# Waits of VectorE on its own results at four places of the tile loop of a two-layer graph network

## The chip, the cores and the metric

The kernel runs on one core of a Trainium2 chip. The metric is the device time of one execution in microseconds (us), from start to end, as the median of several executions. TensorE is PE, VectorE is DVE, ScalarE is ACT, GpSimd is POOL and SyncE is SP in the profile.

## The reference

Two layers pass messages over a graph of 6250 nodes with 206,250 edges (100,000 in both directions and one loop per node), 48 features a node. Shortened to what is computed:

```python
# layer 0
deg = segment_sum(ones, src)                       # self loops added again
h = x + segment_sum(x[src] * rsqrt(deg)[src] * rsqrt(deg)[dst], dst)
h = layernorm(h)
# layer 1
gate = silu(edge_attr @ W1.T + b1) @ W2.T + b2     # 40 -> 48 -> 48, per edge
gate += sum(emb[z[src]] * (emb[z[dst]] @ adaptW.T), -1)
cw = where(d < 6, 0.5 * (cos(pi * d / 6) + 1), 0)
msg = gate * h[dst] * (cw * mult[dst])
agg = segment_sum(msg, src) / segment_sum(mult[dst], src)
out = layernorm(layernorm_affine(h + agg) + h)
```

The edges come sorted by dst.

## The kernel before

The program has three stages. The first (to about 240 us) turns the node and edge lists into keys, counts degrees and fills a table of node rows in HBM (`table`). The second is a loop over NT = 101 tiles of 128 x 16 edges. The third adds up what the loop left in HBM (`slots`) for 51 buckets of nodes and normalizes.

**The tile loop.** `over_tiles` runs a list of steps per engine, each step with a lag: in turn t a step with lag 4 works on tile t - 4. Each engine has a list of its own, in a hand-written order, and executes it strictly in order; semaphores tie the lists together. The steps that matter:

- POOL (L711 to L731) does two things only. `gather` issues 16 indirect DMAs a tile, each of which fetches 128 table rows into `slot` (L718); it first waits until the sums, the gate and the product of the tile six back are done, and for the tile's indices. `scatter` (L726) writes the routed rows of tile t - 6 to `slots` with one indirect DMA. Indirect DMAs are made up by POOL itself.
- SP (L661 to L707) issues the plain loads in the order `index` (the indices of the coming gathers, L666), `load` (edge attributes), `rows`, `weigh`, and from the 47th tile on `early_rows` (L701), which waits until PE's early sum before it is done.
- PE (L863): `layer1`, `pick` (node rows by the one-hot `oh_t`), `layer2`, `routes` (112 matmuls with the one-hots `oh_r`, L815), `early_sum` (21 matmuls with `eoh`, L836), `ranks` (with `oh_b`), and last `total`, the matmul of the gathered rows with the one-hot of dst `oh_d` (L850), which waits for all 16 gathers.
- ACT (L1029) moves results out of PSUM: `ssum` (L898), `got` and `parts` (L943, L949), `routed` (L888), `emine` (L975, the places of the early rows).
- DVE (L1255) makes the one-hots and the products. In a turn, after `normalize` (odd tiles only, a chain of some 17 tiny instructions): `step_at`, `oh_d` (`onehots`, L1041, 128 x 2048 elements), `oh_b` (`buckets`, L1046), eight `oh_r` of 128 x 896 (`route_onehots(0)`, L1083), `sidx`, from the 47th tile on `add_early` and `early_onehots` (L1170: `eoh` in two pieces of 16 and 5 columns), `less_first`, `less_high(0)` (L1209), `product(1)` (L1188 to L1201), `less_second`, `places` (`oh_t`, L1051), `less_high(1)`, `less_middle(0)` (L1217), eight more `oh_r` (`route_onehots(1)`), `less_middle(1)`; then `spots`, `keys` and `product(0)` of the next turn.

**Early rows.** From the 47th tile on, each turn also takes the first 96 of the 256 places of one of the 51 buckets out of `slots`: SP loads them (`erows`), ACT copies the places, DVE makes the one-hot `eoh`, PE sums, ACT copies the sum out, DVE adds it up. The rest of the places is done in the third stage.

**Waits.** `e.wait_ge(sem, n)` holds the engine's next instruction back until the semaphore has come to n. `wait_apart(e, sem, n, passed)` (L80) puts an increment of a semaphore that nobody reads behind the wait. DVE waits for its own results in `product` (`own`, `gate_used`) and `normalize` (`chain`), where one instruction reads what the one before wrote. Between the one-hots it doesn't; there is nothing that the next reads of the last.

## Time and profile before

| | |
|---|---|
| three timed executions | 3001.81, 3028.74, 3037.04 us; median 3028.74 |
| the profiled execution | 3017.23 us, its span in the trace 3015.4 us |
| first gather of the tile loop starts at | 241.60 us |
| last gather of the tile loop starts at | 2712.32 us |
| busy time of DVE, PE, POOL, ACT | 2404.1, 2240.8, 2132.0, 1396.7 us |
| granted clock of TensorE, mean | 0.847 of full speed |

In a timeline row stand the start, the duration, engine, line, operation, what it writes and reads, the shapes, how many instructions were merged (x8), and in brackets the idle time of its engine before it with what ended that. "issue" there means that nothing which the profile shows was waited for. DMA-issuing instructions of POOL are shown with the time that POOL itself spent on them; that the data has landed is shown by who waits for it.

### The profile page before, as it was taken

The page shows a single profiled execution, that of the slowest core. Times are in us where ns is not written, and L with a number is a line of the kernel's source. Part 1 is how long each engine was busy: PE and PEld are TensorE (multiplying, and loading weights), DVE is VectorE, ACT ScalarE, POOL GpSimd, SP SyncE. Part 2 cuts the span into 40 slices and gives each one's busy share as a digit, 9 for nine tenths or more (in the row PEclk, how much of TensorE's full clock was granted, in tenths as well). Part 3 has the DMA queues.
Part 4 walks back from the last instruction along what each step waited for, and adds up shares of the span by engine and source line. Part 5 has one row for each costly group of instructions (what it writes and reads, how often), then busy time and mean ns, then how long its engine had stood idle before and what let it go on. Part 6 is the DMA issues. An engine that isn't in the chain of part 4 may idle for free.

```text
span 3015.4 us, 73281 instructions
## 1 busy us (share of the span) xinstructions
PE 2240.8 (74%) x25807; PEld 1910.9 (63%) x25909; DVE 2404.1 (80%) x5426; ACT 1396.7 (46%) x2928; POOL 2132.0 (71%) x1852
## 2 busy tenths in 40 slices
PE   6980477777777777876787777878778777878675
PEld 5870355566666666665566666766666666767674
DVE  9994477777787877877788888888778878888798
ACT  7982244444444444544444444444444444445123
POOL 7406777877777777778777777777777777770255
PEclk8665688888888878888889898988889988899898
DMA  8405233334444444443344454545445544453896
GB/s 315 156 0 164 62 100 111 111 114 128 116 118 123 113 121 121 118 123 100 109 145 146 144 151 140 159 142 159 132 132 156 153 131 150 146 148 118 336 389 221
DMA packets 167498, 438.96 MB, mean 146 GB/s; under 512 B 85302, under 2 KB 85302, under 8 KB 147446
## 3 DMA queue, kind: packets, MB, share of 16 engines
q1 hardware_dynamic: 96266, 233.49, 23.4%
q0 software_dynamic: 67888, 194.98, 22.4%
q10 hardware_dynamic: 3004, 5.90, 0.6%
q8 instruction: 220, 3.60, 0.5%
q14 instruction: 120, 0.98, 0.1%
HBM read 291.23 MB, written 142.99 MB: 144 GB/s over the span
## 4 chain that ended last, share of the span: by engine, by line
POOL 33%; PE 19%; issue 16%; DVE 14%; DMA 7%; ACT 1%; DVEq 0%; POOLq 0%; ACTq 0%; SPq 0%
POOL slot L718 32%; PE acc L1588 4%; PE route L815 4%; DMA erows<-slots 4%; PE pwin L771 3%; DVE oh_r L1083 3%; DMA slot<-table,gidx 3%; PE phid L741 3%; PE gate L753 2%; PE pwin L850 2%; POOL slots L726 1%; DVE val L1194 1%; DVE eoh L1170 1%; PE pwin L836 1%; DVE val L1197 1%
## 5 line engine op out<-in xcount | busy, mean ns | idle before, releaser
L718 POOL DMA_INDIRECT slot<-table,gidx x1616 | 1819.1, 1126 | 634.2 <-issue 624.7
L815 PEld LDWEIGHTS route<-parts,oh_r 128*128 128x128 bf16 x11312 | 761.7, 99 | 88.1 <-issue 63.5
L815 PE MATMUL route<-parts,oh_r 128*128 128x148 bf16 x11312 | 810.1, 232 | 3.4 <-DVE parts L1217 3.0
L1083 DVE TENSOR_SCALAR oh_r<-iota_r,spot 128x896 bf16<-128x896 f16 x1616 | 613.5, 449 | 69.4 <-PE route L815 69.2
L888 ACT ACTIVATE routed<-route 128x444 bf16<-128x444 f32 (+1 forms) x1010 | 507.9, 513 | 255.1 <-PE route L815 241.6
L850 PE MATMUL pwin<-slot,oh_d 128*128 128x144 bf16 x1616 | 173.5, 282 | 428.1 <-DMA slot<-table,gidx 396.9
L850 PEld LDWEIGHTS pwin<-slot,oh_d 128*128 128x128 bf16 x1616 | 152.4, 156 | 452.2 <-issue 294.1
L771 PEld LDWEIGHTS pwin<-win,oh_t 128*128 128x128 bf16 x4848 | 257.1, 115 | 181.1 <-issue 95.6
L741 PE MATMUL phid<-attr,w 80*96 80x512 f32 x404 | 285.1, 796 | 47.6 <-issue 47.1
L771 PE MATMUL pwin<-win,oh_t 128*128 128x80 bf16 (+1 forms) x4848 | 271.4, 224 | 50.5 <-ACT ssum L898 45.6
L1188 DVE TENSOR_TENSOR prod<-slot,got 128x256 f32<-128x256 f32 x202 | 84.2, 417 | 241.1 <-ACT parts L949 241.1
L753 PE MATMUL gate<-w,hid 97*128 97x96 f32 x1616 | 249.2, 303 | 1.6 <-ACT hid L876 1.6
L943 ACT ACTIVATE got<-pwin 128x640 f32<-128x640 f32 x202 | 142.0, 703 | 221.8 <-PE pwin L771 221.1
L753 PEld LDWEIGHTS gate<-w,hid 97*128 97x128 f32 x1616 | 223.9, 214 | 3.5 <-ACT hid L876 2.8
L726 POOL DMA_INDIRECT slots<-routed,sidx x101 | 119.6, 1184 | 111.3 <-ACT routed L888 73.1
L956 ACT ACTIVATE parts<-val 128x384 bf16<-128x384 f32 x202 | 104.5, 517 | 197.5 <-DVE val L1201 197.5
L876 ACT ACTIVATE hid<-phid,b1c 96x512 f32<-96x512 f32 x202 | 137.6, 681 | 121.9 <-PE phid L741 119.1
L327 ACT ACTIVATE by_col<-oh_hi 128x832 bf16<-128x832 bf16 x101 | 179.4, 1797 | 16.3 <-DVE oh_lo L467 11.6
L1170 DVE TENSOR_TENSOR eoh<-number,emine 128x2048 bf16<-128x2048 bf16 x102 | 102.8, 1057 | 97.0 <-ACT emine L975 96.3
L1588 PE MATMUL acc<-rows,onehot 128*128 128x147 bf16 x1785 | 135.9, 239 | 52.9 <-issue 34.5
L1588 PEld LDWEIGHTS acc<-rows,onehot 128*128 128x128 bf16 x1785 | 130.4, 143 | 58.5 <-issue 58.4
L964 ACT ACTIVATE parts<-val 128x384 bf16<-128x384 f32 x202 | 108.4, 537 | 74.7 <-DVE val L1209 73.4
(226 smaller groups left out, 3221.1 us busy)
## 6 DMA issues: line engine op xcount, KB each, us to landing
rows<-slots SPq DMA_DIRECT2D x51, 1295.0 KB, 9.1
oh_t<-dst_row SPq DMA_DIRECT2D x101, 512.0 KB, 5.5
erows<-slots SPq DMA_DIRECT2D x51, 777.0 KB
attr<-in_edge_attr SPq DMA_DIRECT2D x101, 320.0 KB
slots<-zeros SPq DMA_DIRECT2D x53, 518.0 KB
slot<-table,gidx POOLq DMA_INDIRECT x1616
table<-tab SPq DMA_DIRECT2D x3, 676.0 KB, 5.5
weight_t<-weights SPq DMA_DIRECT2D x101, 8.0 KB
```

Of the source, the lines that this page charges most:

```text
L327: e.activation(by_col[:, s % OR], oh_hi[:, s % OR].rearrange("p b g -> p g b"), ACT.Copy).then_inc(laid, 1)
L718: e.indirect_dma_start(out=slot[:, s, g, :], out_offset=None, in_=table0, in_offset=bass.IndirectOffsetOnAxis(ap=gidx[:, s, g:g + 1], axis ...
L726: e.indirect_dma_start(out=perm, out_offset=bass.IndirectOffsetOnAxis(ap=sidx[:, s:s + 1], axis=0), in_=routed[:, s % 2, :], in_offset=Non ...
L741: e.matmul(phid[:, :], w1[:, :], attr[:, s % 2, 512 * m:512 * (m + 1)], start=True, stop=True).then_inc(hidden, 1)
L753: mm = e.matmul(gate[:, 2 * C * k:2 * C * (k + 1)], hid[:, P * c:P * (c + 1)], w2[:, :], start=True, stop=True)
L771: mm = e.matmul(pwin[:, g // 4, first:first + n], oh_t[:, s % 2, m * HC + g, :], win[:, s, AT[k]:AT[k] + n], start=(k == 0), stop=(k == 2) ...
L815: mm = e.matmul(route[:, (NPH * m + phase) % 2, RC * (j - a):RC * (j - a + 1)], oh_r[:, c, slot_of, :], parts[:, s % 2, c, :], start=(c == ...
L850: mm = e.matmul(sums, oh_d[:, s % 2, :, g], rows[:, g, :], start=(g == 0), stop=(g == G - 1))
L888: e.activation(routed[:, s % 2, RC * (HS * m + a):RC * (HS * m + b)], route[:, (NPH * m + phase) % 2, 0:RC * (b - a)], ACT.Copy).then_inc( ...
L943: e.activation(got[:, m].rearrange("p (b k) c -> p b k c", b=2), by_bank[:, :, :, 0:WX], ACT.Copy)
L1083: oh = e.tensor_scalar(oh_r[:, c], iota_r[:, :, :], spot[:, s % 2, c:c + 1], None, ALU.is_equal)
L1588: mm = e.matmul(acc[:, b % 2, 0:3 * MW], onehot[:, b % OS, :, c], rows[:, b % RS, c, 0:3 * MW], start=(c == 0), stop=(c == COLS - 1))
```

## The change

DVE waits at four places until its own last instruction is done, each time with `wait_apart`: behind `oh_d` (every tile), behind the last `oh_r` of `route_onehots(1)` (every tile), behind `less_high(0)` (every tile), and between the two pieces of `eoh` (51 visits of buckets), for which a semaphore `epart_made` is new. No operand, no size and no order of steps changes.

```diff
--- before.py
+++ after.py
@@ -621,8 +621,8 @@
                                      "ranked", "placed", "routing", "rows_ok_f", "picked",
                                      "got_ok", "gated", "own", "gate_used", "val_ok", "high", "rested_f",
                                      "mid", "split_ok", "stepped", "group_rows", "ones_ok"))
-            erows_in, ecopied, emade, esummed = (
-                sem(n) for n in ("erows_in", "ecopied", "emade", "esummed"))
+            erows_in, ecopied, emade, esummed, epart_made = (
+                sem(n) for n in ("erows_in", "ecopied", "emade", "esummed", "epart_made"))
             (dst_at, all_at, v, a_own, w_ready, w_turned, w_out, rest_ok, weighed, query_r) = (
                 sem(n) for n in ("dst_at", "all_at", "v_p", "a_own_p", "w_ready", "w_turned", "w_out", "rest_ok",
                                      "weighed", "query_r"))
@@ -1040,6 +1040,7 @@
                         e.wait_ge(summed, t - 1)
                     e.tensor_tensor(oh_d[:, s % 2], number[:, :, :], bc_mid(w16[:, bass.ds(t * G, G)], P),
                                     ALU.is_equal).then_inc(ohd, 1)
+                    wait_apart(e, ohd, t + 1, passed)
 
                 def buckets(i, s):
                     t = U * i + s
@@ -1083,6 +1084,8 @@
                             oh = e.tensor_scalar(oh_r[:, c], iota_r[:, :, :], spot[:, s % 2, c:c + 1], None,
                                                  ALU.is_equal)
                         oh.then_inc(ohr, 1)
+                        if m == 1:
+                            wait_apart(e, ohr, 2 * t + 2, passed)
                     return step
 
                 def normalize(i, s):
@@ -1165,10 +1168,13 @@
                     wait_apart(e, ecopied, 2 * v + 1, passed)
                     if not isinstance(v, int) or v > 0:
                         e.wait_ge(esummed, v)
-                    for a in range(0, ECOLS, G):
+                    for k, a in enumerate(range(0, ECOLS, G)):
                         b = min(a + G, ECOLS)
                         oh = e.tensor_tensor(eoh[:, :, a:b], number[:, :, 0:b - a], bc_mid(emine[:, a:b], P),
                                              ALU.is_equal)
+                        if b < ECOLS:
+                            oh.then_inc(epart_made, 1)
+                            wait_apart(e, epart_made, (ECOLS - 1) // G * v + k + 1, passed)
                     oh.then_inc(emade, 1)
 
                 def add_early(i, s):
@@ -1208,6 +1214,8 @@
                         e.wait_ge(high, n + 1)
                         e.tensor_tensor(val[:, m], val[:, m], parts[:, s % 2, m * HC:(m + 1) * HC, 0:C],
                                         ALU.subtract).then_inc(rested, 1)
+                        if m == 0:
+                            wait_apart(e, rested, n + 1, passed)
                     return step
 
                 def less_middle(m):
```

How DVE's queue stands in a turn with early rows. Names are the tiles written and read; `[waits ...]` lists the semaphores that the row waits for; ISA and REGISTER_ALU rows compute addresses and counts. DVE, from the step rows of the groups to the first `oh_r`, before:

```order
L1063 ISA [waits group_rows]
L1063 TENSOR_TENSOR step_at<-iota_f,rstart_t 52x128
L1041 ISA [waits summed_f]
L1041 TENSOR_TENSOR oh_d<-number,w 128x2048
L1046 ISA
L1046 TENSOR_TENSOR oh_b<-number,bkt 128x816
L83 ISA [waits placed]
L1083 TENSOR_SCALAR oh_r<-iota_r,spot 128x896 [waits routing]
```

and now:

```order
L1064 ISA [waits group_rows]
L1064 TENSOR_TENSOR step_at<-iota_f,rstart_t 52x128
L1041 ISA [waits summed_f]
L1041 TENSOR_TENSOR oh_d<-number,w 128x2048
L83 REGISTER_ALU
L1047 ISA [waits ohd]
L1047 TENSOR_TENSOR oh_b<-number,bkt 128x816
L83 ISA [waits placed]
L1084 TENSOR_SCALAR oh_r<-iota_r,spot 128x896 [waits routing]
```

The wait for `ohd`, which `oh_d` increments, now stands behind `oh_d`, ahead of the address computation of `oh_b`.

DVE, from the early one-hots to `product(1)`, before:

```order
L1170 TENSOR_TENSOR eoh<-number,emine 128x128x16 [waits ecopied,esummed]
L1170 TENSOR_TENSOR eoh<-number,emine 128x128x5
L1141 REGISTER_ALU
L1142 TENSOR_TENSOR hm<-hm,win 128x48 [waits win_h]
L1209 TENSOR_TENSOR val<-val,parts 128x384 [waits high]
L1187 REGISTER_ALU
L1188 TENSOR_TENSOR prod<-slot,got 128x256 [waits got_ok]
```

and now:

```order
L1173 TENSOR_TENSOR eoh<-number,emine 128x128x16 [waits ecopied,esummed]
L83 REGISTER_ALU
L1173 TENSOR_TENSOR eoh<-number,emine 128x128x5 [waits epart_made]
L1144 REGISTER_ALU
L1145 TENSOR_TENSOR hm<-hm,win 128x48 [waits win_h]
L1215 TENSOR_TENSOR val<-val,parts 128x384 [waits high]
L1193 REGISTER_ALU [waits rested_f]
L1194 TENSOR_TENSOR prod<-slot,got 128x256 [waits got_ok]
```

The second piece of `eoh` now waits for the first (`epart_made`), and the row ahead of `prod` waits for `val` (`rested_f`).

DVE, from `less_middle(0)` to the next turn's `spot`, before:

```order
L1217 TENSOR_TENSOR parts<-val,parts 128x8x48 [waits mid]
L83 REGISTER_ALU
L1083 TENSOR_SCALAR oh_r<-iota_r,spot 128x896 [waits routing]
L1083 TENSOR_SCALAR oh_r<-iota_r,spot 128x896 x7
L1217 TENSOR_TENSOR parts<-val,parts 128x8x48 [waits mid]
L1056 TENSOR_REDUCE spot<-rank 128x16 [waits ranked]
```

and now:

```order
L1225 TENSOR_TENSOR parts<-val,parts 128x8x48 [waits mid]
L83 REGISTER_ALU
L1084 TENSOR_SCALAR oh_r<-iota_r,spot 128x896 [waits routing]
L1084 TENSOR_SCALAR oh_r<-iota_r,spot 128x896 x7
L1225 TENSOR_TENSOR parts<-val,parts 128x8x48 [waits ohr,mid]
L1057 TENSOR_REDUCE spot<-rank 128x16 [waits ranked]
```

`less_middle(1)`, the second `parts`, now also waits for the last `oh_r` (`ohr`).

## Rows read from the trace of the kernel before

**Rows 1.** The page: the chain that ended last, by engine.
```profile
POOL 33%; PE 19%; issue 16%; DVE 14%; DMA 7%; ACT 1%; DVEq 0%; POOLq 0%; ACTq 0%; SPq 0%
```
**Rows 2.** Groups of POOL by line, 241 to 1670 us, then 1670 to 2712 us.
```profile
L718 POOL DMA_INDIRECT slot<-table,gidx x945 | 1065.7, 1128 | 409.9 <-issue 405.7 <-DVE val L1194 3.7 <-DMA gidx<-src_pid 0.6
L726 POOL DMA_INDIRECT slots<-routed,sidx x53 | 59.8, 1128 | 16.1 <-issue 16.1
...
L718 POOL DMA_INDIRECT slot<-table,gidx x671 | 753.5, 1123 | 224.3 <-issue 219.0 <-DMA gidx<-src_pid 5.0 <-DVE val L1194 0.3
L726 POOL DMA_INDIRECT slots<-routed,sidx x41 | 52.1, 1271 | 12.5 <-issue 11.9 <-DMA gidx<-src_pid 0.6
```
**Rows 3.** The gather's line and the one-hot of dst: durations min/median/max in ns.
```profile
L718 POOL DMA_INDIRECT slot<-table,gidx x1616: 938/1012/5685, 241.6 to 2712.3; - x180
...
L1041 DVE TENSOR_TENSOR oh_d<-number,w x101: 1206/1209/1226, 278.4 to 2674.9; 128x2048 bf16<-128x2048 bf16 x101
```
**Rows 4.** Timeline of POOL: the first and the last gather that start inside an oh_d.
```profile
279.57 1.97 POOL L718 DMA_INDIRECT slot<-table,gidx  x1 [0.30 <-issue]
...
2675.87 1.52 POOL L718 DMA_INDIRECT slot<-table,gidx  x1 [0.30 <-issue]
```
**Rows 5.** Timeline of DVE and POOL around two gathers that start inside oh_d.
```profile
1216.66 1.21 DVE L1041 TENSOR_TENSOR oh_d<-number,w 128x2048 bf16<-128x2048 bf16 x1
1217.11 1.58 POOL L718 DMA_INDIRECT slot<-table,gidx  x1 [0.30 <-issue]
...
1409.05 1.21 DVE L1041 TENSOR_TENSOR oh_d<-number,w 128x2048 bf16<-128x2048 bf16 x1
1409.86 5.67 POOL L718 DMA_INDIRECT slot<-table,gidx  x1 [0.30 <-issue]
1410.19 0.57 DVE L1046 TENSOR_TENSOR oh_b<-number,bkt 128x816 bf16<-128x816 bf16 x1
...
1414.30 0.41 DVE L1188 TENSOR_TENSOR prod<-slot,got 128x256 f32<-128x256 f32 x1
```
**Rows 6.** Waits: who waited for whom, us in total, times, longest us.
```profile
PE pwin L850 <- DMA slot<-table,gidx: 396.9, 94, 18.9
DVE prod L1188 <- ACT parts L949: 241.1, 51, 18.9
DVE eoh L1170 <- ACT emine L975: 96.3, 32, 6.4
PEld pwin L771 <- ACT ssum L898: 74.8, 43, 4.9
DVE oh_r L1083 <- PE route L815: 69.2, 43, 2.9
```
**Rows 7.** Timeline of DVE inside normalize, with waits on its own results.
```profile
1508.53 0.27 DVE L1114 SCALAR_TENSOR_TENSOR y<-y,dinv,base 128x48 f32<-128x48 f32 x1 [0.19 <-DVE y L1113]
...
1509.19 0.18 DVE L1119 BATCH_NORM_AGGREGATE mv<-stat 128x2 f32<-128x6 f32 x1 [0.15 <-DVE stat L1117]
```
**Rows 8.** Timeline around less_high(0) and product(1) without a wait between.
```profile
1267.29 0.55 DVE L1209 TENSOR_TENSOR val<-val,parts 128x384 f32<-128x384 f32 x1
1267.54 1.44 POOL L718 DMA_INDIRECT slot<-table,gidx  x1 [0.30 <-issue]
1267.75 0.41 DVE L1188 TENSOR_TENSOR prod<-slot,got 128x256 f32<-128x256 f32 x1
```
**Rows 9.** Timeline of POOL: a gather that starts inside the last oh_r before less_middle(1).
```profile
2171.06 1.59 POOL L718 DMA_INDIRECT slot<-table,gidx  x1 [0.30 <-issue]
```
**Rows 10.** Timeline of POOL: gathers that start inside the first piece of eoh.
```profile
1517.60 2.52 POOL L718 DMA_INDIRECT slot<-table,gidx  x1 [0.30 <-issue]
...
1540.91 1.93 POOL L718 DMA_INDIRECT slot<-table,gidx  x1 [0.30 <-DMA gidx<-src_pid]
```
**Rows 11.** A late tile: POOL in the timeline, then a piece of the chain.
```profile
2214.65 1.57 POOL L718 DMA_INDIRECT slot<-table,gidx  x1 [2.74 <-issue]
...
2205.72 7.94 DMA erows<-slots
```

## The prediction

> **What bounds the kernel now.** I read the page's shares and its chain first. The page alone misleads: VectorE is busy longest (2404 us in the table above), and the chain gives POOL only 33% and PE 19% [rows 1]. The tile loop runs from the first gather at 241 us to the last at 2712 us, and in it no engine is full by its busy time. So I looked at what POOL does between its instructions. A gather (L718) lasts 0.94 us at least (938 ns [rows 3]), and 0.30 us "issue" stands before it [rows 4, 5]: with rounding, one each 1.25 us. That 0.30 is there before nearly every gather: 945 gathers and 53 scatters in the first stretch take 1065.7 + 409.9 + 59.8 + 16.1 = 1551 us, more than the 1429 us only because the 122 us wait ahead of the first gather is counted; without it, 1429 of 1429. In the second stretch 753.5 + 224.3 + 52.1 + 12.5 = 1042 of 1042, of which 224.3 - 671 x 0.30 = 23 us are real waits [rows 2]. POOL is full by its issue pace. A tile's 16 gathers and a scatter cost 17 x 1.25 = 21.2 us undisturbed, and a tile takes 2471 / 101 = 24.5.
>
> The difference is gathers that last longer than 0.94: min 938, median 1012, max 5685 ns [rows 3]. The mean of 1126 gives (1126 - 940) x 1616 = 300 us in all. I laid the 1616 gathers against VectorE's timeline. A gather that starts inside an instruction of one-input reduction, of `val<-gate,logit` or of the short normalizing ones lasts 0.94. One that starts inside a one-hot or a product with two SBUF inputs lasts longer, by just the time until that instruction is nearly done. Of the 100 that start inside an `oh_d` (the first at 279.57, the last at 2675.87 [rows 4]) the extras add up to 99 us. And the hold does not always end with the instruction. At 1217.11 a gather inside `oh_d` lasts 1.58: taking 0.94 off its end, it was let go at 1217.75, `oh_d` + 1.09; at 1409.86, 0.81 us into the same instruction, one lasts 5.67 and comes free only when `oh_b`, all eight `oh_r`, `sidx`, `hm`, `val` and `prod` have run [rows 5]. There are 8 of these (6 over 5.6 us, 2 over 5.1). Nearly all the instructions it sat through overlap the next one (`oh_d` lasts 1.21, `oh_b` starts at +1.14); it comes free near the end of `prod`, the first of them behind which VectorE waits for its own result.
>
> PE has slack: 397 us of waits for gathers, 94 times, 4.2 a tile. VectorE has (241.1 + 96.3 + 69.2) / 101 = 4.0 us a tile of waits for others [rows 6].
>
> **The change, part by part.** Nothing is removed or reordered. 101 + 51 + 101 + 101 = 354 waits of VectorE on its own last result are added. What is queued behind each: `oh_b`, the second `eoh` piece, `less_middle(1)`, `product(1)`, on which ranks, the early sum, the second half of routes and the gate wait.
>
> *Price of one.* The trace has such waits: `mv` starts 0.15 us after `stat` ends, where a wait and a bare semaphore increment stand between; `y` L1114, with an address to be computed after the wait, starts 0.19 us late [rows 7]. Without a wait the next starts 0.09 us early (1267.29 + 0.55 against 1267.75 [rows 8]). So 0.24 to 0.28, I take 0.25, since in other pairs the overlap is 0.07: 354 x 0.25 = 88 us of VectorE, 0.87 a tile, out of 4.0 of slack. From below a wait could cost nothing, where VectorE would wait for others anyway; from above 0.19 + 0.94, if a gather that slips into the gap held VectorE as long as it runs. The second I hold unlikely: `oh_d` takes 1206 to 1226 ns in all 101 [rows 3], though gathers run across it.
>
> *Gain of one.* I take each gather that is held past the end of an instruction which now gets a wait behind it, and let it go at that end:
> `oh_d` (releases at +1.09): 35 of 56 held gathers in tiles 0 to 58 give 46.7 us, of it 6 x 4.4 + 2 x 3.4 = 33 from the eight long ones; 21 of 41 later give 10.4.
> `less_high(0)` before `product(1)`: 16 gathers, all like the one at 1267.54, 1.44 long [rows 8], 0.3 each: 5.0, all in the first part.
> The last `oh_r` before `less_middle(1)`: like 2171.06, 1.59 long [rows 9]: 12 give 4.9, 9 later give 3.7.
> Between the `eoh` pieces: at 1517.60 a gather is held through both (2.52), at 1540.91 only through the first (1.93) [rows 10]: 3 give 1.8 early, 7 later 5.3.
> Sum: 58.4 us in tiles 0 to 58, 19.4 after. That is a replay with unchanged phases. If gathers fell at random (an arrival inside `oh_d` then waits 1.09 / 2 with chance 1.09 / 1.25, so 0.48 us a tile against 0.99 now) the whole first part would give 45. I take 52.
>
> *Who is late next.* In the first part (to about 1670 us) POOL never waits, and PE has its 4.2 us a tile. VectorE's 4.0 less 0.87 less about 0.9 of gain leaves 2.2, so POOL stays the bound and the 52 us arrive. From the sixtieth tile a ring of another kind is about as slow as POOL: early sum, SP's early rows, their DMA (7.9 us at 2205.72 [rows 11]), `emine`, `eoh` (96 us idle before it [rows 6]), `less_high(0)`, `product(1)`, ScalarE, `pick`, early sum. There the gathers' index load hangs behind SP's early rows, POOL itself waits 2.74 us at 2214.65 [rows 11]; PE's loads wait so 43 times, 74.8 us [rows 6]. 27 of the 39 tiles 59 to 97 have this idle. Two of the added waits lie on that ring (in `eoh`, behind `less_high(0)`): + 0.5 us a tile. Where it decides (27 tiles) + 13 us and nothing of the 19 comes; where POOL decides a third of 19 comes. I put the second part at + 0, from - 19 to + 20. After the last gather the loop drains five tiles through PE and VectorE, of whose chain VectorE is under half: 5 x 0.87 x 0.6 = + 3 us. The last stage is untouched.
>
> Sum: - 52 + 0 + 3 = - 49. The profiled execution took 3017.2 us (span 3015.4): 2968. The median shown is 3028.7, 11.5 above it, in a spread of 35; I put the forecast between 2968 and 3028.7 - 49 = 2980, at 2975, 1.8% down.
>
> **A rule that speaks against it.** In the trace a gather is delayed by `oh_d`, a TENSOR_TENSOR of VectorE [rows 5]. The Trainium skill (SBUF — State Buffer, Who interferes with whom) says that a two-input VectorE instruction contends with GpSimd instructions that read SBUF, and infers that descriptor generation, which writes, is spared by `tensor_tensor`; it also says that the loser is blocked for the whole instruction, no longer. By the first nothing would be gained at `oh_d` and `eoh`; the trace disagrees (99 us in 100 gathers). By the second a gather goes free when the instruction ends, wait or none, and the gain is nil; the trace agrees for 1217.11 and disagrees for 1409.86. This second is a rival below.
>
> **The rivals.**
> *The late ring takes it back.* For it: the 23 us that POOL already waits, and the 43 waits for `ssum`. Against: 59 tiles lie ahead of it. First part - 45, second + 0.6 x 39 = + 23, drain + 4: 3017 - 18 = 2999, and 3011 by the median.
> *The gap frees nothing.* What keeps a gather out for 4.7 us could be its own retry or a phase, not the missing gap. For it: at + 0.70 in `oh_d` gathers are released at + 1.09 with the same overlap, at + 0.81 not. Against: no gather that starts in `val` L1197 or `prod`, which have a self-wait behind them, is held longer than 0.42. Then only the price is left: ring + 0.3 x 39 = 12, drain 4: 3017 + 16 = 3033.
> *VectorE becomes the bound (slower).* If a gather in the gap keeps the port for its 0.94 us, each wait costs 1.19, 3.5 x 1.19 = 4.2 us a tile. It decides from 4.0 a tile on in the first part, at once in the ring. Second part + 2 x 1.19 x 39 = + 93, first + 0.2 x 59 = + 12, less a gain of 45, drain + 12: 3017 + 72 = 3089. Against it: `oh_d`'s constant duration.
>
> **The numbers.** Forecast 0.60, late ring 0.20, nothing freed 0.13, VectorE bound 0.07. A measurement of this kernel can tell about 1%, 30 us: faster means under 2998. The forecast lies there but for 0.04, of the late ring 0.08: together 0.64. Slower (over 3059) has the last rival and a little of the third: 0.09. Within 1%: 0.27. The range takes - 19 in the second part and 58 in the first as its low end (2940), the late ring and part of "nothing freed" as the high one (3030).
>
> **What the profile after would show.** Right: the longest gather drops from 5.7 to about 2 us, the mean of L718 from 1126 to 1080 ns, gathers inside `oh_d` end by + 1.09, `oh_b` starts 0.15 to 0.2 after `oh_d` ends, the loop ends near 2665. The ring shows as POOL's "issue" idle above 0.30 and waits for `ssum` growing after 1650 us. Wrong: gathers still held past `oh_d` (nothing freed); `oh_b`, `prod` starting 0.9 late or VectorE's waits for others near zero (VectorE bound).

## The result, and the profile after

The changed kernel takes 3043.9 us (median of 20 runs, 3029.0 to 3049.4), the kernel before 3029.5 us (20 runs, 3001.8 to 3037.0). The ratio is 1.0051, with a 95% interval of [1.0036, 1.0067]: half a per cent slower, where 1.8% faster was forecast. 3043.9 lies outside the predicted range of 2940 to 3030.

The page of the changed kernel, first its chain by engine, which answers to [rows 1], then groups of instructions with busy time, mean ns of one, and the idle time before them:

```profile
POOL 28%; PE 19%; DVE 19%; issue 16%; DMA 7%; ACT 2%; DVEq 1%; SPq 0%; ACTq 0%; POOLq 0%
...
L718 POOL DMA_INDIRECT slot<-table,gidx x1616 | 1770.5, 1096 | 697.4 <-issue 658.0
...
L1084 DVE TENSOR_SCALAR oh_r<-iota_r,spot 128x896 bf16<-128x896 f16 x1616 | 605.3, 446 | 55.2 <-PE route L815 55.2
```

POOL has lost 5 points of the chain and VectorE has won 5. A gather lasts 1096 ns on average instead of 1126, so the gathers as such became 48 us cheaper in all. POOL's groups by line, 241 to 1635 us and then 1635 to 2702 us, answer to [rows 2]:

```profile
L718 POOL DMA_INDIRECT slot<-table,gidx x944 | 1025.4, 1086 | 411.7 <-issue 409.2 <-DVE val L1200 2.1 <-DMA gidx<-src_pid 0.3
L726 POOL DMA_INDIRECT slots<-routed,sidx x53 | 59.1, 1115 | 16.1 <-issue 16.1
...
L718 POOL DMA_INDIRECT slot<-table,gidx x656 | 725.8, 1106 | 278.2 <-issue 241.2 <-DMA gidx<-src_pid 37.0
L726 POOL DMA_INDIRECT slots<-routed,sidx x42 | 48.8, 1162 | 12.8 <-issue 12.8
```

In the first stretch the gathers' busy time fell from 1065.7 to 1025.4 us and nothing else grew by over 2 us: POOL is still full by its issue pace but for 6 us, and the gain arrives. In the second the gathers are shorter too (1106 against 1123 ns), but POOL's idle time is now 278.2 - 656 x 0.30 = 81 us above the pace, where it was 23 us. POOL is no longer always the bound there. The stretches of the loop side by side, divided at the first gather of the tiles with index 51, 59 and 100 (us, and behind the counts the granted clock); first the changed kernel:

```profile
240.89:1438.26 1197.37, 856.48 (x9741) 716.78 (x9741) 903.62 (x2254) 529.13 (x1166) 935.00 (x861) 0.84 0.41 118
1438.26:1635.45 197.19, 153.15 (x1770) 130.35 (x1769) 158.77 (x383) 87.67 (x205) 149.51 (x137) 0.88 0.46 138
1635.45:2702.41 1066.96, 840.32 (x9431) 720.66 (x9428) 858.55 (x2049) 466.87 (x1089) 773.59 (x698) 0.85 0.47 139
```

and the kernel before at the same tiles:

```profile
241.60:1474.30 1232.70, 859.87 (x9690) 721.09 (x9739) 904.35 (x2265) 531.46 (x1168) 970.30 (x861) 0.84 0.40 114
1474.30:1669.92 195.62, 153.97 (x1803) 130.49 (x1809) 158.44 (x383) 89.67 (x205) 154.16 (x136) 0.89 0.47 140
1669.92:2688.87 1018.95, 814.34 (x9348) 693.26 (x9389) 842.63 (x2039) 466.87 (x1084) 786.74 (x697) 0.87 0.49 146
```

The loop starts 0.7 us earlier and reaches tile 59 after 1394.6 instead of 1428.3 us. With the earlier start that is 34.5 us won at tile 59. The 41 tiles behind it take 1067.0 instead of 1019.0 us: 48.0 lost. From there to the end another 7.0 are lost. - 34.5 + 48.0 + 7.0 = + 20.5, the difference of the two spans (3035.9 and 3015.4).

Durations in ns (min/median/max), which answer to [rows 3]:

```profile
L718 POOL DMA_INDIRECT slot<-table,gidx x1616: 938/954/3474, 240.9 to 2725.3; - x180
...
L1041 DVE TENSOR_TENSOR oh_d<-number,w x101: 1206/1209/1226, 277.9 to 2690.7; 128x2048 bf16<-128x2048 bf16 x101
```

Of the ten gathers over 3 us one is left, in the drain. Laid against VectorE's timeline, 95 gathers start inside `oh_d`, with 57.7 us of extra time (before: 100 with 99.2), and none of them has more than 0.97 us extra (before: up to 4.73). The four added waits in one late tile, the timeline of VectorE, answer to [rows 5, 7, 8]:

```profile
1704.19 0.58 DVE L1047 TENSOR_TENSOR oh_b<-number,bkt 128x816 bf16<-128x816 bf16 x1 [0.25 <-DVE oh_d L1041]
...
1715.28 0.88 DVE L1173 TENSOR_TENSOR eoh<-number,emine 128x640 bf16<-128x640 bf16 x1 [0.15 <-DVE eoh L1173]
1716.76 0.42 DVE L1194 TENSOR_TENSOR prod<-slot,got 128x256 f32<-128x256 f32 x1 [0.22 <-DVE val L1215]
1724.14 0.56 DVE L1225 TENSOR_TENSOR parts<-val,parts 128x384 bf16<-128x384 f32 x1 [0.15 <-DVE oh_r L1084]
```

With the overlap that is gone (0.07 to 0.09) a wait costs 0.32 behind `oh_d`, 0.31 behind `less_high(0)`, 0.23 to 0.29 at the other two. And at the end of some loop turns there is something that no row of before had led me to expect. VectorE's timeline there, and the same with the line of `spot` as a whole:

```profile
1617.76 1.53 DVE L1084 TENSOR_SCALAR oh_r<-iota_r,spot 128x896 bf16<-128x896 f16 x4
1619.45 0.56 DVE L1225 TENSOR_TENSOR parts<-val,parts 128x384 bf16<-128x384 f32 x1 [0.15 <-DVE oh_r L1084]
1622.65 1.01 DVE L1057 TENSOR_REDUCE spot<-rank 128x16 f32<-128x816 f32 x1 [2.64 <-issue]
...
  issue: 31.8, 11
```

`spot` is the first instruction of a loop turn of six tiles. 11 times VectorE stands idle for 2.4 to 4.9 us ahead of it, waiting for nothing that the profile shows, 31.8 us in all; before it did so 3 times, for 2.3 us. The 11 are the tiles with index 18, 24, 30, 36 and then 54, 60 and so on to 90. For VectorE `over_tiles` writes out the first 17 tiles' turns and 6 in the middle one by one, and puts the others into two loops of 5 and of 8 turns of six tiles: there are 11 jumps back, and the idle stretches stand behind just these. The rows of waits, last, answer to [rows 6]:

```profile
PE pwin L850 <- DMA slot<-table,gidx: 288.8, 78, 18.5
...
DVE prod L1194 <- ACT parts L949: 154.2, 26, 19.0
PE pwin L771 <- ACT ssum L898: 150.1, 54, 5.7
PEld pwin L771 <- ACT ssum L898: 131.8, 48, 5.5
...
DVE eoh L1173 <- ACT emine L975: 102.2, 33, 5.8
```

PE's waits for gathers shrink by 108 us, and its weight loads' waits for `ssum` grow from 74.8 to 131.8 us. I read that as the ring of the late part (early sum, early rows, `eoh`, `less_high(0)`, `product(1)`) coming later than POOL more often than before.

### The profile page after: what moved, and what is told of

Read it like the earlier page. It is cut to its first block, busy times and chain, and to the rows that moved or that the text cites. A ratio compares the mean times of both kernels' runs of the same rounds, so it can differ in the third digit from the quotient of the medians.

```text
span 3035.9 us, 73850 instructions
## 1 busy us (share of the span) xinstructions
PE 2263.1 (75%) x25909; PEld 1936.3 (64%) x25909; DVE 2422.0 (80%) x5426; ACT 1390.8 (46%) x2928; POOL 2079.4 (68%) x1852
## 4 chain that ended last, share of the span: by engine, by line
POOL 28%; PE 19%; DVE 19%; issue 16%; DMA 7%; ACT 2%; DVEq 1%; SPq 0%; ACTq 0%; POOLq 0%
POOL slot L718 27%; DMA erows<-slots 5%; PE route L815 5%; PE acc L1596 4%; DVE oh_r L1084 4%; PE pwin L771 4%; DVE eoh L1173 3%; PE gate L753 2%; PE phid L741 2%; DVE val L1200 1%; PE pwin L836 1%; POOL slots L726 1%; DVE val L1203 1%; DVE logit L1197 1%; DVE prod L1194 1%
## 5 line engine op out<-in xcount | busy, mean ns | idle before, releaser
L718 POOL DMA_INDIRECT slot<-table,gidx x1616 | 1770.5, 1096 | 697.4 <-issue 658.0
L1084 DVE TENSOR_SCALAR oh_r<-iota_r,spot 128x896 bf16<-128x896 f16 x1616 | 605.3, 446 | 55.2 <-PE route L815 55.2
L771 PEld LDWEIGHTS pwin<-win,oh_t 128*128 128x128 bf16 x4848 | 283.4, 124 | 270.4 <-ACT ssum L898 131.8
L771 PE MATMUL pwin<-win,oh_t 128*128 128x80 bf16 (+1 forms) x4848 | 298.9, 237 | 155.7 <-ACT ssum L898 150.1
L850 PE MATMUL pwin<-slot,oh_d 128*128 128x144 bf16 x1616 | 151.9, 259 | 320.8 <-DMA slot<-table,gidx 288.8
L850 PEld LDWEIGHTS pwin<-slot,oh_d 128*128 128x128 bf16 x1616 | 136.1, 151 | 341.8 <-issue 200.3
L741 PE MATMUL phid<-attr,w 80*96 80x512 f32 x404 | 271.1, 759 | 49.3 <-issue 37.8
L753 PE MATMUL gate<-w,hid 97*128 97x96 f32 x1616 | 267.3, 318 | 1.6 <-ACT hid L876 1.6
L753 PEld LDWEIGHTS gate<-w,hid 97*128 97x128 f32 x1616 | 241.5, 229 | 3.3 <-ACT hid L876 2.8
L1173 DVE TENSOR_TENSOR eoh<-number,emine 128x2048 bf16<-128x2048 bf16 x102 | 109.5, 1073 | 110.1 <-ACT emine L975 102.2
```

The lines of the kernel that those rows point to most:

```text
L718: e.indirect_dma_start(out=slot[:, s, g, :], out_offset=None, in_=table0, in_offset=bass.IndirectOffsetOnAxis(ap=gidx[:, s, g:g + 1], axis ...
L741: e.matmul(phid[:, :], w1[:, :], attr[:, s % 2, 512 * m:512 * (m + 1)], start=True, stop=True).then_inc(hidden, 1)
L753: mm = e.matmul(gate[:, 2 * C * k:2 * C * (k + 1)], hid[:, P * c:P * (c + 1)], w2[:, :], start=True, stop=True)
L771: mm = e.matmul(pwin[:, g // 4, first:first + n], oh_t[:, s % 2, m * HC + g, :], win[:, s, AT[k]:AT[k] + n], start=(k == 0), stop=(k == 2) ...
L850: mm = e.matmul(sums, oh_d[:, s % 2, :, g], rows[:, g, :], start=(g == 0), stop=(g == G - 1))
L1084: oh = e.tensor_scalar(oh_r[:, c], iota_r[:, :, :], spot[:, s % 2, c:c + 1], None, ALU.is_equal)
```

## The experiments

All kernels below are the changed kernel with a condition on its four waits. `in_late` is true in the loops that also serve the early rows, from tile `EARLY_FROM`. Ratios are to runs of the kernel before on the same chip. Chips and medians of before: 3019.6 us for the first four kernels and again, on a second chip, for the next four.

| kernel | waits left | median us | ratio and interval |
|---|---|---|---|
| changed | all four | 3043.9 | 1.0051 [1.0036, 1.0067] |
| first_only | `oh_d`, `oh_r`, `less_high(0)`; early part only | 2998.5 | 0.9935 [0.9910, 0.9960] |
| late_off | `oh_d`, `oh_r`; late part only | 3037.7 | 1.0056 [1.0030, 1.0082] |
| late_on | `eoh`, `less_high(0)`; late part only | 3040.8 | 1.0069 [1.0043, 1.0094] |
| ohd_only | `oh_d`, all tiles | 2994.5 | 0.9923 [0.9898, 0.9948] |
| ohr_last | `oh_r`, last tile of a turn | 3028.0 | 1.0040 [1.0017, 1.0064] |
| ohr_others | `oh_r`, the other five tiles | 3032.9 | 1.0060 [1.0037, 1.0082] |
| four_others | all but `oh_r` in the last tile | 3020.9 | 1.0014 [0.9991, 1.0037] |
| best_a | `oh_d` all; `less_high(0)` and `oh_r` (not the last tile) early only | 2972.3 | 0.9859 [0.9831, 0.9887] |

**Which part, which waits.**

```diff
# first_only (the eoh wait is taken out)
-                    wait_apart(e, ohd, t + 1, passed)
+                    if not in_late(i, s):
+                        wait_apart(e, ohd, t + 1, passed)
...
-                        if m == 1:
+                        if m == 1 and not in_late(i, s):
                             wait_apart(e, ohr, 2 * t + 2, passed)
...
-                        if m == 0:
+                        if m == 0 and not in_late(i, s):
                             wait_apart(e, rested, n + 1, passed)
```

> The three waits of every tile stand only in tiles 0 to 46, before the early rows begin; none stands later. Theory ring (the first part is bound by POOL, and the gain there is real; the late part loses it): the stretch up to the 52nd tile's first gather takes 1197 us as in the changed kernel (1233 before), the rest is as before, about 1.2% under the kernel before (2995). Rival run (the 35 us of the first part are only a chance of phase, and the late part makes up for a POOL that is ahead by waiting more): no faster than before, 3025 to 3035, with POOL's waits above 0.30 grown in the late part.

Measured: 0.65% faster (0.9935), 2998.5 us. With the waits of the early part alone the change gains; the tiles behind 59 lose nothing (1009.5 us, taken as above). The mark of 1197 us up to tile 51 was missed: 1217.4, some half of the gain, because the waits end at tile 45.

```diff
# late_off (less_high(0) and eoh waits are taken out)
+                    if in_late(i, s):
                         wait_apart(e, ohd, t + 1, passed)
...
-                        if m == 1:
+                        if m == 1 and in_late(i, s):
                             wait_apart(e, ohr, 2 * t + 2, passed)
```

> Only in the late tiles (from the 47th on), and only the two waits that do not lie on the ring of the early rows: behind oh_d and behind the last oh_r. Theory ring (only what lies on early sum, load, emine, eoh, less_high(0), product(1), pick counts): these two cost nothing, 3029, within 0.3% of before. Rival queue (in the late part VectorE's whole queue is the bound, every wait is paid in full wherever it stands): 0.31 + 0.23 us a tile, 54 tiles, +29 us less 10 of gathers let go: +20 to +29, 3050 to 3058.

```diff
# late_on (oh_d and oh_r waits are taken out, the eoh wait stays)
-                        if m == 0:
+                        if m == 0 and in_late(i, s):
                             wait_apart(e, rested, n + 1, passed)
```

> Only in the late tiles, and only the two waits on the ring: between the pieces of eoh and behind less_high(0). Theory ring: 0.29 + 0.31 us a tile, 51 tiles, +30 us, and since the changed kernel lost 48 us there, up to +48: 3059 to 3077. Rival queue: +30 us, 3059, and together with the run with the other two waits the sum makes up the changed kernel's late loss.

```diff
# ohd_only (the other three are taken out)
                     wait_apart(e, ohd, t + 1, passed)
```

> Only the wait behind oh_d, in all tiles. The replay gave 80% of the first part's gain to it. Theory ring: 27 us gained early, nothing lost late: 3002, 0.9% under before. Rival queue: 27 gained, 0.31 x 54 = 17 lost: 3019, 0.3% under. In both no gather that starts inside oh_d lasts over 2.05 us.

Measured: late_off 0.56% and late_on 0.69% slower than before, ohd_only 0.77% faster. late_off was expected within 0.3% by the one theory and at + 20 to + 29 us by the other, and late_on at + 30 or more by both: neither theory foresaw + 17 and + 21. ohd_only came out as the theory of the ring had it, with 27.4 us gained at tile 59 and no gather inside `oh_d` over 1.9 us. So both pairs of waits lose in the late part, and not by way of `oh_d`: with its wait alone the last 41 tiles take 1016.6 us, not more than before. first_only, late_off and late_on divide the change's waits among them, each wait in just one: 0.9935 x 1.0056 x 1.0069 = 1.0060, and the changed kernel has 1.0051 [1.0036, 1.0067]. The three effects add up: - 20, + 17 and + 21 us. The wait behind `oh_d` stands in late_off from tile 46 on, so part of the early gain is in it: tile 59 starts 16.6 us earlier than before in first_only, 15.8 in late_off and 34.5 in the changed kernel. Two causes were left: the pair on the ring, as the prediction had it, and the wait behind the last `oh_r`, which it had put at no loss. In late_off's trace the idle stretch ahead of `spot` stood again, and what followed it. First VectorE, then PE, then POOL, and the stretch from 1653.80 us with its granted clock (0.58):

```profile
1642.78 1.01 DVE L1066 TENSOR_REDUCE spot<-rank 128x16 f32<-128x816 f32 x1 [2.48 <-issue]
...
1645.54 0.42 DVE L1203 TENSOR_REDUCE logit<-prod 128x8 f32<-128x256 f32 x1 [1.34 <-issue]
...
1653.31 0.58 PE L808 MATMUL rank<-delta_t,step_at 52*128 x2 [4.69 <-DVE step_at L1073]
1653.82 6.34 PE L823 MATMUL route<-parts,oh_r 128*128 128x148 bf16 x56
...
1686.90 1.54 POOL L726 DMA_INDIRECT slot<-table,gidx  x1 [8.70 <-DMA gidx<-src_pid]
...
1653.80:1660.20 6.40, 6.36 (x57) 6.28 (x59) 5.28 (x13) 2.17 (x6) 4.87 (x6) 0.58 0.81 277
```

The same two rows of PE in the kernel before, where the granted clock is 1.00:

```profile
1660.81 0.38 PE L800 MATMUL rank<-delta_t,step_at 52*128 x2 [1.87 <-DVE step_at L1063]
1661.13 3.87 PE L815 MATMUL route<-parts,oh_r 128*128 128x148 bf16 x56
```

VectorE loses 3.8 us, PE idles 4.69 us for `step_at` (before 1.87), the granted clock is 0.58 in the next 6.4 us (near the 1.2 GHz level), and 56 routing matmuls take 6.34 us, 113 ns each (before 3.87 us, 69 ns). POOL's tile 59 lasts 32.8 us instead of 23.6, since at its end POOL waits 8.70 us for its indices. Tiles 59, 65, 77, 83 and 95, five of the seven with index 59, 65 and so on to 95, last 31.8 to 33.1 us in that run.

**The wait at the loop's branch.** The step behind the last `oh_r` of the sixth tile is the last but one of the turn; only `less_middle(1)` stands between its wait and the branch back.

```diff
# ohr_last (the other three are taken out)
-                        if m == 1:
+                        if m == 1 and s == U - 1:
```

> Only the wait behind the last oh_r, and only in the tile whose step stands last in the loop's body (one in six, 17 waits in all, 14 of them right before the branch back). Theory branch: with the wait VectorE's queue is empty when its sequencer comes to the branch, so the branch and the fetch of the next instructions lie bare: 2.4 to 2.7 us idle before spot in each of the 14 turns of the loop, and in the late part the PE behind it idles, its clock falls and a tile of 30 us or more follows; 0.5 to 1% slower, 3035 to 3050. Rival: every wait costs its 0.23 us wherever it stands, 17 x 0.23 = 4 us: 3022 to 3026, no idle before spot.

```diff
# ohr_others (the other three are taken out)
-                        if m == 1:
+                        if m == 1 and s < U - 1:
```

> Only the wait behind the last oh_r, in the other five tiles of six (84 waits). Theory branch: no idle before spot; 84 x 0.23 us are in part hidden, 9 us of gathers let go: within 0.3% of before. Rival (no place is special): five times the effect of the run with the waits in the sixth tile alone, and most of the 26 us a tile of the late part in the run with the two waits off the ring (late tiles 25.5 and more).

```diff
# four_others (the other three stay)
-                        if m == 1:
+                        if m == 1 and s < U - 1:
```

> The changed kernel with one kind of wait left out: behind the last oh_r of the tile that stands last in the loop's body. Theory branch: the first part keeps its gain (52nd tile's first gather at 1440), the late tiles take 25.2 to 25.5 us instead of 26.0, from the two waits on the ring; 3005 to 3020, 0.2 to 0.8% under before and 0.8 to 1.2% under the changed kernel. Rival (the late loss is the sum of all waits): as the changed kernel but for 4 us, 3040.

Measured: the waits at the turn's end alone (ohr_last) cost 0.40%, a little less than the 0.5 to 1% of the theory. The tiles that stand last in a turn have index 5, 11 and so on to 95, so there are 16 such waits and 85 others, not 17 and 84, and 11 of the 16 stand ahead of a jump back, not 14. The idle ahead of `spot` by kernel, the rows of what its engine sat idle for: ohr_last, then first_only; before and the changed kernel had 2.3 us 3 times and 31.8 us 11 times:

```profile
  issue: 27.9, 11
...
  issue: 12.7, 6
```

ohr_others, ohd_only and best_a have no such idle stretch. Taking the 16 waits out of the changed kernel (four_others) brings it from 1.0051 to 1.0014, and its last 41 tiles from 1067.0 to 1049.2 us; 7 stretches of about 1 us are left there. Two comparisons, 0.40 and 0.37%, thus put 11 or 12 us on those 16 waits. That is a rough size: the first has an interval of 0.17 to 0.64%, the second compares ratios from two chips, and by the medians alone ohr_last is 0.28% slower. The four idle stretches of the early part cost nothing: ohr_last reaches tile 59 at 1667.3 us, before at 1669.9. four_others was expected at 3005 to 3020 us and 0.8 to 1.2% under the changed kernel; it took 3020.9, and the tiles behind 59 take 25.6 us each, not 25.2 to 25.5.

Why at that place? VectorE's sequencer can only reach the branch when the wait is over. The row of the queue q14, whose few transfers I take for VectorE's instructions by their times, in the changed kernel from 1620.40 to 1620.90 us, and then in the kernel before from 1797 to 1799 us:

```profile
q14 instruction: 1, 0.01, 7.0%
```

```profile
q14 instruction: 1, 0.01, 1.5%
```

Each is the last one ahead of `spot`; others come some us apart. In the changed kernel it comes 1.1 us after the wait is over, and `spot` starts 2.1 us behind it, at 1622.65. In the kernel before it comes near 1797.95, while the eight `oh_r` still run, and `spot` starts at 1800.15 with an idle of only 0.24. In another turn before, it comes near 1649.25, and `spot` is 1.14 late at 1651.16. In the traces of both kernels the last transfer on q14 ahead of `spot` lies 1.9 to 2.2 us ahead of it at each of the 11 jumps back, with a wait or without; of the other 90 tiles only 3 in each trace have one within 3 us. The wait only decides whether that time lies beside `oh_r` or behind it. The Trainium skill (Runtime: NRT & Kernel Launch, Instruction fetch mechanics) says that a taken branch whose target isn't in the window of two blocks forces a fetch before execution can go on. The trace agrees, with 1.9 to 2.2 us a time and with 11 jumps back for 11 stretches. Two of the stretches are longer, 4.86 and 4.13 us at tiles 18 and 30, in one trace of the changed kernel; what was added there is not known.

What it costs in the late part can be read off POOL. 30 to 50 us behind each of the seven late jumps back POOL has a wait, in all but a few cases for its indices; 0.30 us of each is its pace. The sum of the longest wait there behind each of the seven, beside the time of the 41 tiles behind 59, one trace each:

| kernel | 41 tiles, us | seven waits, us |
|---|---|---|
| before | 1019.0 | 5.9 |
| late_on | 1032.5 | 4.7 |
| four_others | 1049.2 | 16.2 |
| ohr_last | 1024.0 | 18.6 |
| changed | 1067.0 | 34.6 |
| late_off | 1066.0 | 49.1 |

So 43 of the 47 us that late_off loses there, and 29 of the changed kernel's 48, stand behind the jumps back. The 13 us in ohr_last show in its 41 tiles only as 5. Why the same idle stretches of some 2.5 us cost POOL more with other waits beside them isn't shown; PE's idle time ahead of `step_at` is on average 3.4 us in the seven turns of ohr_last and 4.3 in those of late_off, against 1.6 before.

ohr_others was a miss: 0.60% slower, where the waits were expected to do little. It has no stretch ahead of `spot`, and its late part is sound (24.6 us a tile). It loses in the early part: tile 59 starts at 1684.4 us instead of 1669.9, because its gathers fall worse (their extra time over 0.94 is 3.74 us a tile against 3.25 in tiles 4 to 22, and over the whole loop 16 of them last over 3 us, where it was 10). I read it so: a wait that lets a few gathers go also shifts VectorE against POOL's beat, and here the shift lost more than the 4.9 us that the replay gave for the release. With the wait behind `oh_d` beside it, as in best_a below, no such loss shows.

**The version that beats both.**

```diff
# best_a, against the changed kernel (the eoh wait is taken out)
-                        if m == 1:
+                        if m == 1 and s < U - 1 and not in_late(i, s):
                             wait_apart(e, ohr, 2 * t + 2, passed)
...
-                        if m == 0:
+                        if m == 0 and not in_late(i, s):
                             wait_apart(e, rested, n + 1, passed)
```

> oh_d's wait in all tiles, the ones behind less_high(0) and the last oh_r in tiles before the early rows only, the latter not at the loop's end, none in eoh. If the parts add up: 35 us gained early, 5 late: 2980 to 2990, 1.0 to 1.3% under before. Rival: the extra waits of the first part add nothing to oh_d's, 2994 as with oh_d's alone.

Measured: 2972.3 us, 0.9859 of before. Its two stretches, to tile 59 and from there to tile 100:

```profile
241.00:1631.62 1390.62, 1009.38 (x11543) 846.35 (x11544) 1065.13 (x2641) 620.15 (x1371) 1086.77 (x998) 0.85 0.42 121
1631.62:2634.57 1002.95, 804.62 (x9394) 685.70 (x9392) 844.76 (x2043) 467.42 (x1086) 771.44 (x698) 0.90 0.50 148
```

It is better than the 2980 to 2990 expected. It keeps all of the early gain (38 us, where ohd_only has 27) and takes 16 us less than before in the late part, at a granted clock of 0.90 instead of 0.87; but this trace is of the fastest of its six runs.

**Eight runs that told little.** The next four kernels were to split the pair on the ring, to set 17 waits behind `oh_r` away from the branch as a control, and to take the `oh_r` waits out of best_a:

```diff
# ohr_s0 (the other three are taken out)
+                        if m == 1 and s == 0:
# eoh_only: the wait between the eoh pieces alone
# high_late (the other three are taken out)
+                        if m == 0 and in_late(i, s):
# best_b: best_a without the waits behind oh_r
```

> Only the wait behind the last oh_r, and that only in the first of the six tiles of a loop turn (17 waits, as many as stood at the turn's last tile in the run before, which took 0.40% longer than the kernel before and showed VectorE 11 times idle 2.5 us ahead of spot). Theory branch back (the wait right ahead of the loop's branch costs, not the wait as such): no idle of 2 us ahead of spot, ratio to before 0.998 to 1.001. Rival (17 waits at this place of the step cost 0.4% wherever they stand, by the phases that they shift): ratio 1.003 to 1.005 again, without the idle.

> Only the wait between the two eoh pieces of the early tiles (51 waits). Theory ring (each wait on the ring of the late part delays its turn by the wait's own price, 0.3 us): 39 x 0.3 = 12 us less up to 5 us of gathers let go earlier, ratio to before 1.002 to 1.004. Rival one (the wait behind less_high(0) carries the whole loss of the run that had both, 0.69%): ratio 1.000 or below, since the gathers that were held through both pieces now end with the first. Rival two (this wait carries all of it): 1.006 to 1.007.

> Only the wait behind less_high(0), and only in the late tiles (about 43 waits). Theory ring: 39 x 0.3 = 12 us, ratio to before 1.003 to 1.005. Rival one (this wait carries the whole loss of the run that had both): 1.006 to 1.007. Rival two (the eoh wait does): 1.000.

> The wait behind oh_d in all tiles and that behind less_high(0) in the early part alone; none in eoh, none behind oh_r. It is the fastest version so far (ratio 0.9859) less its waits behind oh_r in the early part. Theory A (each wait that lets gathers go adds its gain, 4.9 us for the oh_r waits of the first part by the replay): ratio 0.987 to 0.988. Rival B (the oh_r waits alone lost 13 us in the first part by the phases, and would do so here too): ratio 0.981 to 0.983. Rival C (the gains are not additive at all, the phases decide): 0.990 or above, near the 0.9923 of the oh_d waits alone.

They and their repetition fell on a chip on which the kernel before itself took 4018 and then 4079 us. Ratios, first round and second:

| kernel | ratio | again |
|---|---|---|
| ohr_s0 | 1.0002 [0.9968, 1.0037] | 1.0023 [0.9982, 1.0065] |
| eoh_only | 0.9975 [0.9933, 1.0017] | 0.9986 [0.9936, 1.0037] |
| high_late | 0.9976 [0.9935, 1.0018] | 1.0032 [0.9990, 1.0074] |
| best_b | 1.0114 [1.0060, 1.0168] | 1.0121 [1.0059, 1.0183] |

There the loop is bound by something else, as far as the traces of these runs show (the kernel before has none from that chip). ScalarE and then VectorE in ohr_s0:

```profile
1495.94 0.28 ACT L957 ACTIVATE parts<-pwin 128x24 bf16<-128x24 f32 x1
1515.99 0.70 ACT L951 ACTIVATE got<-pwin 128x640 f32<-128x640 f32 x1 [19.77 <-remote]
...
1522.10 2.27 DVE L1093 TENSOR_SCALAR oh_r<-iota_r,spot 128x896 bf16<-128x896 f16 x6 [16.28 <-PE route L823]
```

```profile
ACT got L951 <- remote: 750.0, 95, 20.5
```

ScalarE stands 20 us in front of one evacuation and releases VectorE late; 95 waits of that kind, up to 20.5 us long, make 750 us. In the first trace of ohr_s0 none of VectorE's 19 idle stretches over 0.6 us without a releaser stands ahead of `spot`, as a cost of the branch alone would have it; but a loop bound by ScalarE proves little. No ratio of that chip can be carried over to the loop near 3020 us, and what holds ScalarE there is not known. That best_b, the wait behind `oh_d` in front, takes 1.2% more there is a fact of that chip, and it was not tried whether best_a does too.

> The same kernel as in the run high_late, which fell on a chip where the kernel before too took 4018 us. Only the wait behind less_high(0), in the late tiles alone (about 43 waits). Theory ring: 39 x 0.3 = 12 us, ratio to before 1.003 to 1.005. Rival one (this wait carries the whole loss of the run that had both): 1.006 to 1.007. Rival two (the eoh wait does): 1.000.

> The same kernel as in the run eoh_only. Only the wait between the two eoh pieces (51 waits). Theory ring: 39 x 0.3 = 12 us less up to 5 us of gathers let go, ratio 1.002 to 1.004. Rival one (the less_high(0) wait carries all): 1.000 or below. Rival two (this wait carries all): 1.006 to 1.007.

> The same kernel as in the run ohr_s0. The wait behind the last oh_r in the first tile of each loop turn alone (17 waits). Theory branch back: no idle of 2 us ahead of spot, ratio 0.998 to 1.001. Rival (17 such waits cost 0.4% wherever they stand): 1.003 to 1.005 without that idle.

> The same kernel as in the run best_b. The wait behind oh_d everywhere and that behind less_high(0) in the early part, none behind oh_r. Theory A (gains add up): ratio 0.987 to 0.988. Rival B (the oh_r waits lost by their phases): 0.981 to 0.983. Rival C (the phases decide): 0.990 or above.

**The two main kernels again.** The last two runs went to another chip, where the kernel before took 3011.2 us.

> The same kernel as in the run best_a, which took 0.9859 of the kernel before near 3020 us. Near 3020 us again: 0.983 to 0.989. On a chip where the kernel before takes 4020 to 4080 us (as in the last eight runs, where best_b took 1.011 and 1.012 of it): theory A (there POOL is not the bound, gathers let go bring nothing, and the waits are left with their price): 1.005 to 1.015, like best_b. Theory B (the oh_r waits of the first part, which best_b lacks, make the difference): 0.99 to 1.00.

> The changed kernel itself once more. Near 3020 us: 1.004 to 1.007 as before. On a chip where the kernel before takes 4020 to 4080 us: theory A (waits of VectorE cost their price where ScalarE's idle stretches bound the loop, gathers gain nothing): 1.010 to 1.020, as it has more waits than best_b. Theory B (VectorE has slack there and the waits are hidden): 0.998 to 1.003.

Measured: best_a 2975.2 us, 0.9876 [0.9853, 0.9899]; the changed kernel 3039.2 us, 1.0089 [1.0054, 1.0124]. Both verdicts hold; best_a falls in the 0.983 to 0.989 expected, the changed kernel above its 1.004 to 1.007. Tile 59 starts at 1627.3 and 1630.7 us in the two traces. The changed kernel needs 1071.7 us for the last 41 tiles (1067.0 in its first trace) and again has 11 idle stretches ahead of `spot`, 28.0 us. best_a has none, and needs 1031.3 us where its first trace had 1003.0, so a single trace of the late part is good to some 15 us either way, and the medians have to carry the verdict.

## Why the prediction was wrong

**What bounds the kernel: right.** POOL is full by its issue pace up to tile 59, and gathers let go earlier there shorten the kernel. One reading was off: PE's 396.9 us of waits in 94 times are 4.2 us a wait and 3.9 a tile; nothing hangs on it.

**Price of a wait, 0.24 to 0.28: nearly right.** 0.23 to 0.32 was measured.

**The mechanism: right.** A gather held through a run of overlapping VectorE instructions is let go at the first gap. Holds inside `oh_d` end within 0.97 us of extra time, and `oh_d` still lasts 1206 to 1226 ns. With that the rivals "the gap frees nothing" and "VectorE becomes the bound" fall; the rule of one whole instruction, which the prediction had weighed, does too. (The Trainium skill, SBUF — State Buffer, Who interferes with whom, says of VectorE's two-port modes that whoever issues first gets the shared pair for the whole instruction; that a hold inside `oh_d` follows it, and lasts no longer, was the prediction's own reading.)

**Gain of the early part, - 52: the sign right, the size too large.** The trace shows 34.5 us, that of the repeated run 39.2. It also comes back in parts: 16.6 with the waits up to tile 45 alone (first_only), 15.8 with those from tile 46 on (late_off). The replay let gathers go with unchanged phases; in fact every gather behind a freed one moves, and new ones start badly. The term for `oh_d` was 46.7 us in tiles 0 to 58, and the extra time at `oh_d` fell there by 40.9; over all gathers of these tiles it fell by 39.2, where the replay had 58.4. By the instruction they start in, over the whole loop, extra time at `oh_d` fell by 41.5 and at `eoh` by 13.6 us; at the product with the weight (`val<-val,weight_t`) it rose from 4.4 to 29.9, at `parts<-val,parts` from 22.8 to 33.7, and `hm<-hm,win` is new with 8.4; at `val<-val,got` it fell from 21.2 to 2.5. The prediction's own check, 45 us for gathers that fall at random, was nearer, and ohr_others shows that such a wait can even lose.

**The late part, + 0 from - 19 to + 20: this step failed.** It cost 48.0 us in the trace and 52.8 in that of the repeated run. Already the prediction's own terms, + 13 for the ring and a third of 19 against it, give + 7 and not + 0. Two terms were wrong.
First, and the larger, a term that was not in the sum: what is queued behind the wait at the end of the turn. The text names `less_middle(1)` there and stops. Behind that stands the loop's branch, and behind the branch a fetch that had lain beside eight `oh_r` (3.0 us). VectorE idles some 2.5 us for it at each of 11 jumps back, and behind the seven late ones POOL's waits grow by 29 us in the changed kernel. ohr_last loses 0.40% by it, and four_others wins 0.37% back.
Second, the ring. The prediction put its two waits, 0.5 us a tile, at + 13 us where the ring decides, and set part of POOL's gain against it. late_on, which has just these two waits, is 0.69% slower, 21 us; in its trace the 41 tiles take 1032.5 against 1019.0 us, and 5.0 more are lost before tile 59. The + 13 itself was thus near; the gain set against it did not come: the extra time of late_on's gathers behind tile 59 rose by 8 us, and POOL's waits above its pace by 6. How the two waits share the loss stays open.
What the single traces give for the last 41 tiles does not add up: 1016.6 with `oh_d`'s wait, 1024.0 in ohr_last, but 1066.0 in late_off, which has the wait behind every late `oh_d` and every late last `oh_r`. Part of it is which run was traced: late_off's is the slowest of its eight, 13 us above the median, ohr_last's is 7 under the median. The rest, some 20 us, no run here assigns; no run has `oh_d`'s wait and the one ahead of the branch alone.

**The drain, + 3: not settled.** From the first gather of tile 100 to the end the changed kernel takes 7.0 us more in one trace and 3.1 in the other.

**The rivals.** "The late ring takes it back", with a chance of 0.20, came nearest: its first part of - 45 against - 34.5, its late + 23 against + 48.0, its drain of + 4 against + 7.0. That it came near is in part luck, since it knew nothing of the branch: it was mis-sized in both directions and ended 33 us short of the measured median, by its figure of 3011. The range's high end stood on it.

**Marks named beforehand.** The mean of a gather was to fall to 1080 ns (1096), the longest to about 2 us (3.47, in the drain, and under 3 in the loop), `oh_b` was to start 0.15 to 0.2 late (0.25), the loop's last gather near 2665 us (2725.3, from 2712.3), POOL's "issue" idle and the waits for `ssum` to show the ring (they do).

## What to carry to other kernels

A wait of VectorE for its own last result costs 0.2 to 0.3 us and opens a gap in which POOL's gathers get through; here it pays where POOL's pace is the bound, behind `oh_d` above all (0.77% alone) and with the two other places in the early part 1.41%. Every such wait is to be judged place by place: on the late ring two of them, 0.6 us a tile by their price, cost 0.69%, and ahead of a loop's branch one uncovers the fetch of the loop's first instructions, some 2.5 us a time. Count the jumps back in the program first: they tell how often. When naming what is queued behind a wait, go on past the next instruction to the branch.

## What was not expected of the hardware

- At each of the 11 jumps back of the loop an instruction transfer on q14 lies 1.9 to 2.2 us ahead of the turn's first instruction. In the kernel before, 8 of the 11 show no idle time of VectorE ahead of it; with the wait ahead of the branch all 11 do, 2.4 to 4.9 us.
- Idle time of 4.69 us on PE was followed by a stretch with a granted clock of 0.58 and routing matmuls at 113 ns apiece, where before 1.87 us were followed by 1.00 and 69 ns. In the seven late turns of late_off PE idles 3.2 to 5.3 us there and the granted clock behind it is 0.54 to 0.75; before, 0.7 to 2.5 us and 0.73 to 1.00. That the idle time made the clock fall is my reading of this.
- Chips differ: the kernel before takes 3011 to 3030 us in four sets of runs, and 4018 and 4079 us in the two on another chip, where the trace of ohr_s0 has ScalarE idle up to 20.5 us at a time; small ratios from one regime say nothing on the other.
